# A transformer layer stack on one core: reordering one attention pipeline step and merging its small score products

## The reference

```python
q = (x @ wq_w.T + wq_b).reshape(b, t, H, HD)          # H = 32, HD = 32
k1, v1 = k[:, :, 0, :], v[:, :, 0, :]                 # one head for all queries
scores = jnp.einsum('bqhd,bkd->bhqk', q, k1) / jnp.sqrt(jnp.float32(HD))
scores = jnp.where(causal, scores, -jnp.inf)
weights = jax.nn.softmax(scores, axis=-1)
attn = jnp.einsum('bhqk,bkd->bqhd', weights, v1).reshape(b, t, H * HD)
return attn @ wo_w.T + wo_b
```

## Time and profile before

| | |
|---|---|
| median of 3 runs | 2968.11 us (2965.56 to 2970.6) |
| profiled execution | 2960.29 us, span 2958.6 us, mean granted clock 0.962 |
| busy: TensorE products | 2734.2 us, 92% |
| busy: VectorE | 1678.4 us, 57% |
| busy: ScalarE | 1157.6 us, 39% |
| busy: GpSimd | 949.3 us, 32% |
| the step loop | about 60 us to 1600 us of the span |

### The profile page before, as it was taken

The page is one execution under the profiler, slowest core; times in us unless marked ns, Lnnn a source line. Parts: engine busy times, 40 slices in busy tenths (PEclk is TensorE's granted clock), DMA queues, the critical chain, the costliest instruction groups (busy, mean ns, idle before and its releaser), DMA issues. The chain is left out here.

```text
span 2958.6 us, 41828 instructions
## 1 busy us (share of the span) xinstructions
PE 2734.2 (92%) x15104; PEld 2000.9 (68%) x15104; DVE 1678.4 (57%) x4305; ACT 1157.6 (39%) x2509; POOL 949.3 (32%) x1460
## 2 busy tenths in 40 slices
PE   4888999999999999999998987999999999999988
PEld 3556667667566676676665565777777777777766
DVE  3563464653745645537445256666666666666653
ACT  3663454562744645627446012222222222222220
POOL 2433122221231222212312144535353545444422
PEclk8898999999999999999999988999999999999989
DMA  5765545444535454445344520020202020202001
GB/s 157 200 175 150 171 103 165 120 113 148 129 83 174 106 160 114 116 138 137 87 146 129 187 63 1 1 58 1 57 1 58 1 57 1 58 1 57 3 27 29
DMA packets 103631, 272.29 MB, mean 92 GB/s; under 512 B 12122, under 2 KB 23514, under 8 KB 101122
## 3 DMA queue, kind: packets, MB, share of 16 engines
q1 hardware_dynamic: 102706, 269.55, 33.6%
q10 hardware_dynamic: 720, 0.07, 0.0%
HBM read 168.40 MB, written 50.33 MB: 74 GB/s over the span
## 5 line engine op out<-in xcount | busy, mean ns | idle before, releaser
L664 DVE CUSTOM_DVE_ANT_0 ps_attn<-ps_attn,later_keys 128x512 f32<-128x512 f32 (+3 forms) x1024 | 485.7, 512 | 398.4 <-PE ps_attn L837 396.4
L474 POOL TENSOR_SCALAR_AFFINE_SELECT pt<-pt 128x512 f32<-128x512 f32 x256 | 165.4, 648 | 901.3 <-ACT pt L561 900.1
L561 ACT ACTIVATE pt<-ps_attn 128x512 f32<-128x512 f32 (+1 forms) x704 | 385.9, 560 | 98.6 <-PE ps_attn L865 86.9
L1561 PE MATMUL ps_mixer<-m_w_hi,m_xt_hi 128*128 128x512 f32 x1024 | 416.9, 407 | 1.6 <-DVE m_xt_lo L1343 1.6
L576 ACT ACTIVATE ps_attn<-ps_attn,top 128x512 f32<-128x512 f32 (+1 forms) x512 | 312.7, 611 | 248.6 <-DVE top L664 247.4
L1563 PE MATMUL ps_mixer<-m_w_lo,m_xt_hi 128*128 128x512 f32 x1024 | 400.0, 391 | 0.0
L1562 PE MATMUL ps_mixer<-m_w_hi,m_xt_lo 128*128 128x512 f32 x1024 | 399.6, 390 | 0.0
L865 PE MATMUL ps_attn<-q_stack,k_stack 97*128 97x512 f32 (+3 forms) x1024 | 313.8, 360 | 34.4 <-DMA q_stack<-top_rows 23.1
L837 PE MATMUL ps_attn<-k_stack,q_stack 96*128 96x512 f32 (+3 forms) x1024 | 304.8, 350 | 39.9 <-DMA q_stack<-q_lo 16.0
L1243 ACT CAST m_xt_hi<-ps_mixer 128x512 fp32r<-128x512 f32 x192 | 103.7, 589 | 505.4 <-PE ps_mixer L1556 505.0
L837 PEld LDWEIGHTS ps_attn<-k_stack,q_stack 96*128 96x128 f32 x1024 | 174.4, 194 | 130.0 <-ACT ps_attn L576 72.7
(11 more groups left out here) (216 smaller groups left out, 4945.2 us busy)
## 6 DMA issues: line engine op xcount, KB each, us to landing
xr<-in_a_x SPq DMA_DIRECT2D x64, 512.0 KB, 6.6
q_stack<-q_hi SPq DMA_DIRECT2D x128, 256.0 KB, 5.6
wq_hi<-wq_split SPq DMA_DIRECT2D x56, 512.0 KB, 4.0
wq_lo<-wq_split SPq DMA_DIRECT2D x56, 512.0 KB, 4.6
q_stack<-q_lo SPq DMA_DIRECT2D x64, 256.0 KB, 6.8
wo_hi<-wo_split SPq DMA_DIRECT2D x8, 2048.0 KB, 8.1
wo_lo<-wo_split SPq DMA_DIRECT2D x8, 2048.0 KB, 12.7
x<-xr SPq DMA_DIRECT2D x32, 512.0 KB, 2.8
```

Of the source, the lines that this page charges most:

```text
L561: nc.scalar.activation(pt[k][:, heads[0]:heads[0] + len(heads), :].rearrange("p j t -> p (j t)"), ps[:, ST0 + n % 2, 0:width * len(heads)] ...
L664: mm = nc.vector.tensor_tensor_reduce(part, part, later_keys[:, T - width:T], 1.0, NO_SCORE, ALU.add, ALU.min, top[:, j * TILES + i:j * TI ...
L1561: nc.tensor.matmul(out, a_hi, b_hi, start=first, stop=False)
```

## The change

Five edits, all in the attention's step loop.

1. ScalarE: `finish_high` of step M moves behind `copy_rows` of step M+1, unless step M ends with an output projection.
2. TensorE: score unit 0 of the next group moves ahead of `weigh_first`.
3. TensorE: `shares` hands the query chunks out earlier: 3 and 4 behind score unit 2, 5 to 7 behind score unit 3, none behind score unit 4.
4. ScalarE's `q_high` moves from behind u = 2 to behind u = 1, and VectorE's `q_low` from behind maxima 5 to behind maxima 4, except in step 6 of a batch.
5. TensorE: the turned products of a unit with two or four heads become one instruction of 512 columns that reads the heads through a two-level pattern: 5 products fewer a group.

```diff
                     if inside(M):
                         copy_rows(M)
+                    if output_run(M - 1) is None:
+                        for G in finishes(M - 1):
+                            finish_high(G)
...
-                        if u == 2 and inside(M + 2) and M != -1:
+                        if u == (2 if second is not None else 1) and inside(M + 2) and M != -1:
                             q_high(M + 2)
...
-                    for G in finishes(M):
-                        finish_high(G)
+                    if output_run(M) is not None or M == STEPS[-1]:
+                        for G in finishes(M):
+                            finish_high(G)
...
                     if inside(M + 1):
-                        tops(M + 1, (4, 5))
+                        tops(M + 1, (4, 5) if second is not None else (4,))
                     if inside(M + 2) and M != -1:
                         q_low(M + 2)
                     if inside(M + 1):
-                        tops(M + 1, (6, 7))
+                        tops(M + 1, (6, 7) if second is not None else (5, 6, 7))
...
-                    for m, j in enumerate(heads):
-                        mm = nc.tensor.matmul(ps[:, ST0 + n % 2, m * width:(m + 1) * width], k_stack[:, b % 2, k * P:(k + 1) * P],
-                                              q_stack[:, G % 3, j, k * P:T], start=(m == 0), stop=(m == len(heads) - 1))
-                    mm.then_inc(st_ready, 1)
+                    nc.tensor.matmul(ps[:, ST0 + n % 2, 0:width * len(heads)].rearrange("p (j t) -> p j t", t=width),
+                                     k_stack[:, b % 2, k * P:(k + 1) * P], q_stack[:, G % 3, heads[0]:heads[0] + len(heads), k * P:T],
+                                     start=True, stop=True).then_inc(st_ready, 1)
...
-                    shares = ((0, 1, 2, 3, 4), (5, 6), (7,), (), (), ()) if M == -1 else ((0,), (1,), (2,), (3,), (4, 5), (6, 7))
+                    shares = ((0, 1, 2, 3, 4), (5, 6), (7,), (), (), ()) if M == -1 else ((0,), (1,), (2,), (3, 4), (5, 6, 7), ())
...
+                    if inside(M + 1):
+                        scores(M + 1, 0)
                     if inside(M - 1):
                         weigh_first(M - 1)
-                    if inside(M + 1):
-                        scores(M + 1, 0)
```

## The result

The changed kernel takes 2941.78 us (median of 4 runs, 2937.39 to 2943.31) against 2966.84 us for the kernel before beside it: ratio 0.9915, 95% interval 0.9894 to 0.9935. The forecast was 2959.9 with a range of 2945 to 2973. The direction is right, the size a third of what came. The profiled execution of the changed kernel has a span of 2935.6 us and a mean granted clock of 0.967; before it was 2958.6 and 0.962. Two executions, of 8974 and 12958 us, are left out of all comparisons, and one of 2987 us at a mean clock of 0.903 stands in the ratio of its run but not in the table of executions further down.

The account below looks back on a forecast made before the run. TensorE's order was taken to bound a plain step up to score unit 6, then VectorE's tail. Terms -6.2, +4.9, +2.5 and -9.4 sum to -8.2 us: 2952.1 profiled, 2959.9 for the runs, range 2945 to 2973.

Parts of the forecast that it names:

- What bounds a step: Plain step: TensorE's order rules up to score unit 6, then a 5.7 us VectorE tail; the division delays `weigh_first`; T0 0.23 us earlier.
- The landing of the queries: Stacking DMA of the queries, start of the next step: lands 0.29 us in, down from 1.05, so unit 0 waits 0.06 at most.
- Two signs that were to show the prediction wrong: Plain steps getting shorter, or score unit 0 seen waiting for q_stack, would prove the prediction wrong.
- The hole: VectorE's tail: `q_low` delays maxima 5, so score unit 7 waits 0.41 us; steps 2 and 7 lose 0.35, steps 3 to 5 0.12.
- Merged products and T0 in output steps: Output steps: merging saves 0.33 us of a possible 0.61; with T0's 0.23, step 0 gains 0.56 and step 1 0.33.
- Step 6: Step 6 of a batch: no 0.69 us wait for `copy_rows` and 0.66 less queueing, 1.35 us gained, seven times -9.4.
- The sum: All batches' steps together: -8.2 us, giving 2952.1 on the profiled execution and 2959.9 for the runs.
- the clock stays up: Rival, head of step 6: less idle keeps the clock up, 10 us more gained, 2949; chance 0.07.
- the shifted maxima: `copy_rows` moved first, 1.12 to about 0.34 us into the step: T0 does not wait for it, so gain 0.
- No hole: Rival, VectorE's tail in plain steps: maxima 5 gets through in time, -18 us in all, 2950; chance 0.20.
- Late queries: Rival, step start: unit 0 waits for queries landing 1.05 us in; 28 steps lose 0.7 each, 2980; chance 0.14.
- No effect in step 6: Rival, step 6: the next wait takes the gain back, +9.4 us, 2969; chance 0.17.

## Why the prediction was wrong in size, point by point

- **What bounds a step.** Right: the wait ahead of `weigh_first` was the division (shown when unit 0 is put back), the tail is VectorE's, and T0 moved by 0.26 (forecast 0.23) in M = 51. In steps 2 and 7, where the new place of unit 0 was put at nothing, T0 comes 0.06 later (3.62 to 3.68 us in M = 50).
- **The landing of the queries.** Right: 0.29 forecast, 0.20 measured in M = 51; and 1.05 forecast for the old place, 1.11 for unit 0 without the chunks up. Two signs that were to show the prediction wrong did appear, both small: unit 0 waits 0.05 to 0.12 us for `q_stack` in eight steps of the profile, and steps 3 and 4 are shorter by 0.04.
- **The hole.** It is there, in front of unit 7, for row sum 5, at the time that was worked out: unit 7 later by 0.34 from T0 (forecast 0.41), maxima 7 at 8.03 (forecast 8.09). Two things failed. The cause was put on maxima 5 behind the low part alone, and row sum 5 does follow maxima 5 by the least distance that was reckoned with, 0.65; but ScalarE, whose high part was said to be hidden because the reader of the exponential has 0.7 us to spare, gets to row sum 5 only 0.09 earlier when the low part stands back. The reader of the exponential had the time; the row sums queued behind it had not. And less of the delay reaches the end of a step: from T0 to the next step's start it is 0.21 (12.91 to 13.12 in M = 50), not 0.35, and steps 2 and 7 lose 0.25 with their later T0. Over fourteen steps that is +3.5 for +4.9; in steps 3 to 5 the two effects cancel, -0.2 in all for +2.5.
- **Merged products and T0 in output steps.** -0.53 and -0.26 for -0.56 and -0.33. Right; merging was 0.1 too large there. In plain steps it was put at 0, which holds for the usual step only: merging alone brings M = 34 and 42 from 17.8 us to 16.75 and 16.86, since T0 no longer waits for the shifted maxima.
- **Step 6.** -1.30 for -1.35 at the same clock, and each of its two halves shown apart. Right. With the clock as it came, the seven steps 6 fell by 12.6 us in the mean of the profiles (220.5 to 207.9), where the sum had 9.4.
- **The sum.** The step that failed is that two terms were put at nothing. One is the clock: "the sum leaves it out". The rival "the clock stays up" had 0.07 and was worked out for the head of step 6 alone, up to 10 us there. Most heads keep their half clock, since the 2.14 us ahead of the turned maxima stay, but that of M = 14 runs at the full clock in all three profiles of the changed kernel, and over the program 24 us of half clock went, worth an estimated 7 to 10. The other is the shifted maxima: "T0 does not wait for it in this step, so the gain is 0" was read from M = 51 and is right there (landed at 3.22 us, T0 at 4.11), but not in M = 9, 34, 42 and 57, where T0 waited 1.06 to 1.08 us; about 5 us of such waits went. The lower end of the range, 2945, took in the clock or the missing hole, each by itself; the measured 2941.78 lies below it. The trace of before had the numbers for both: at a clock of 0.962 its span held some 225 us at the half clock, and T0 waited 5.9 us for the transfer, and no term of the sum drew on either.
- **Rivals.** No hole: false, 16.80. The clock: true in part, as above (its time follows from the sum as 2950, not 2949). Late queries: false for this kernel, true without the chunks up. No effect in step 6: false.
- **Luck.** That the direction came out is not luck: the usual steps give -11.4 us where the sum had -8.2, and the 3 us more come from the hole, which was smaller. What went beyond them comes, as far as is known, from the two terms that were left out.

## What to carry to other kernels

When an instruction moves up on an in-order engine, follow all that queues behind it until the next hand-over of a bank, not only its own reader: the high part passed its reader in time and held up a row sum three instructions later. Sum step by step, but then ask what idle time goes or stays in front of dense work, and price the half-clock time of the span as a term with a range of its own: by the estimate above it was about as large here as the whole forecast. Read a wait in every step of its kind and not in one: the transfer that was in time in M = 51 was late in four other steps. An edit that is worth nothing in its step can be what keeps another from costing: without the chunks one place up all the gain was lost.

## What the runs showed of the hardware that was not expected

- Eight products without use in 2.1 us of TensorE's idle time raised the granted clock of the next four us from 0.69 to 1.00, and that step took 28.46 instead of 29.82 us; in two of six steps a stretch at the half clock then came 18 us later.
- A transfer of 8 KB inside the core landed 1.8 to 2.3 us after its issue in a usual step and up to 4.2 us after it in steps where a load of instructions was in flight beside it; without such a load it never took more than 2.4 us from step 9 on.
- The undisturbed plain and output steps repeat within 0.03 us from execution to execution in most kinds; spans of the kernel before ran from 2950.4 to 2973.2. So a difference of 0.1 us in such a step can be read from one profile, while the time of the program needs many runs.
